# Order of the down product's chunks in an expert layer on one core

## The reference, cut to what matters

```
z = 2.0 * buf
z = z * jax.lax.rsqrt(jnp.mean(z * z, axis=-1, keepdims=True) + EPS) * norm_w[:, None, :]
g, u = jnp.split(jnp.einsum('ecd,ehd->ech', z, w13), 2, axis=-1)
y = buf + ALPHA * jnp.einsum('ech,edh->ecd', jax.nn.silu(g) * u, w2)
```

## Time and profile before

| what | value |
|---|---|
| median of 3 runs | 341.99 us (341.45 to 344.46) |
| the profiled execution, its own time | 343.51 us |
| its span, first to last instruction | 341.7 us |
| its mean granted TensorE clock | 0.925 of full speed |

### The profile page before, as it was taken

How to read it: one execution, slowest core, us unless ns; L and a number is a source line. 1 busy time by engine, 2 the same in 40 slices (tenths; PEclk the granted TensorE clock), 3 DMA queues, 4 the chain that set the end, 5 groups by cost and what they waited for, 6 DMA issues and landing times.

```text
span 341.7 us, 6143 instructions
## 1 busy us (share of the span) xinstructions
PE 285.1 (83%) x1893; PEld 226.0 (66%) x1893; DVE 203.8 (60%) x605; ACT 157.5 (46%) x442; POOL 141.6 (41%) x174
## 2 busy tenths in 40 slices
PE   8747889999979798988773939999999999999910
PEld 4624666776767575756562428989899898989910
DVE  2344787788798797978847223654737374564210
ACT  0013667777767575756633025353543535352210
POOL 9313233325545354544546700072433617153360
PEclk9975999999999999999955878999999999999985
DMA  7969700000000000050000181566585757661321
GB/s 246 272 153 304 278 3 0 2 1 12 27 4 25 11 18 18 18 119 24 21 18 28 54 227 26 125 130 175 91 213 105 177 127 141 155 115 11 32 26 17
DMA packets 24843, 30.32 MB, mean 89 GB/s; under 512 B 3346, under 2 KB 21560, under 8 KB 24692
## 3 DMA queue, kind: packets, MB, share of 16 engines
q1 hardware_dynamic: 18275, 21.45, 24.1%
q0 software_dynamic: 6288, 8.49, 12.0%
q10 hardware_dynamic: 256, 0.10, 0.1%
HBM read 19.61 MB, written 11.20 MB: 90 GB/s over the span
## 4 chain that ended last, share of the span: by engine, by line
PE 50%; ACT 13%; DMA 11%; DVE 10%; issue 8%; POOL 5%; ACTq 0%; POOLq 0%; DVEq 0%; SPq 0%
PE bank L541 12%; PE bank L436 6%; ACT kbd L625 6%; DMA zs<-slots 4%; PE bank L518 3%; PE bank L525 3%; PE bank L522 3%; PE bank L519 3%; PE bank L526 3%; DMA slots<-rows,slot 3%; PE bank L468 2%; DMA h_all<-ptok_sb 2%; ACT qT L627 2%; DVE mx L815 2%; PE bank L503 2%
## 5 line engine op out<-in xcount | busy, mean ns | idle before, releaser
L1042 POOL DMA_INDIRECT out_rows<-yw,tok x32 | 51.6, 1613 | 86.4 <-ACT yw L671 79.1
L541 PE MATMUL bank<-w_sb,hT 128*120 128x192 f32 x256 | 43.4, 328 | 1.1 <-DVE hT L928 0.7
L990 POOL TENSOR_TENSOR qk<-rc,rs 128x192 f32<-128x192 f32 x32 | 18.7, 602 | 60.6 <-DVE rs L831 60.6
L541 PEld LDWEIGHTS bank<-w_sb,hT 128*120 128x120 f32 x256 | 41.4, 183 | 2.5 <-issue 2.4
L928 DVE TENSOR_TENSOR hT<-sg,bank 128x480 f32<-128x480 f32 x32 | 20.8, 650 | 34.6 <-ACT sg L662 34.6
L1026 POOL DMA_INDIRECT slots<-rows,slot x32 | 32.3, 1010 | 9.9 <-issue 9.3
L662 ACT ACTIVATE sg<-bank 128x480 f32<-128x480 f32 x32 | 18.3, 571 | 32.7 <-PE bank L526 31.1
L671 ACT ACTIVATE yw<-yx,zs 120x192 f32<-120x192 f32 x32 | 12.8, 448 | 36.2 <-DVE yx L940 36.1
L625 ACT COPY kbd<-bank 32x288 f32<-32x288 f32 x64 | 24.8, 388 | 7.7 <-PE bank L476 6.5
L518 PE MATMUL bank<-z0h,wah 128*128 128x480 f32 x64 | 25.8, 403 | 0.0
L436 PE MATMUL bank<-kbd,qT 128*64 128x192 f32 x192 | 20.1, 347 | 6.4 <-ACT qT L627 6.0
(11 more groups left out here) (143 smaller groups left out, 658.7 us busy)
## 6 DMA issues: line engine op xcount, KB each, us to landing
rawa_sb<-in_w SPq DMA_DIRECT2D x8, 512.0 KB
rawb_sb<-in_w SPq DMA_DIRECT2D x16, 256.0 KB
w_sb<-in_w SPq DMA_DIRECT2D x8, 384.0 KB
slots<-zero_sb POOLq DMA_DIRECT2D x1, 3030.0 KB
zs<-slots SPq DMA_DIRECT2D x8, 378.8 KB
patch_sb<-in_patches SPq DMA_DIRECT2D x1, 1152.0 KB, 7.2
out_rows<-h_all SPq DMA_DIRECT2D x2, 432.0 KB, 5.6
h_all<-in_txt SPq DMA_DIRECT2D x2, 384.0 KB, 8.9
```

The lines of the kernel that those rows point to most:

```text
L541: mm = pe.matmul(bank[6 + c // 2][0:CR, (c % 2) * D:(c % 2 + 1) * D], hT[:, m, c * CR:(c + 1) * CR], w2_sb[:, par, m, :], start=(m == 0), ...
L1042: pool.indirect_dma_start(out=out, out_offset=bass.IndirectOffsetOnAxis(ap=tok[:, e, c:c + 1], axis=0), in_=yw[:, c, :], in_offset=None, b ...
```

## The change

The order in which the chunks of the down product are computed. Before: chunk 0 with m = 0 to 2, chunk 2 with m = 0 to 2, then m = 3 of chunk 0, m = 3 of chunk 2, then chunk 1 and chunk 3 whole. After: chunk 0 with m = 0 to 2, its m = 3, chunk 1, then chunk 2, then chunk 3. The waits are written by the part and the chunk: the wait for hT[3] stands ahead of chunk 0's m = 3 as before, the wait for the second bank to be free stands ahead of chunk 2's first matmul as before, and `s_down` is raised behind chunks 1 and 3 as before. Number, shape and operands of the matmuls are the same.

```diff
-                for c, parts in ((0, (0, 1, 2)), (2, (0, 1, 2)), (0, (3,)), (2, (3,)),
-                                 (1, (0, 1, 2, 3)), (3, (0, 1, 2, 3))):
+                for c, parts in ((0, (0, 1, 2)), (0, (3,)), (1, (0, 1, 2, 3)),
+                                 (2, (0, 1, 2, 3)), (3, (0, 1, 2, 3))):
                     if parts[0] == 0 and c == 0:
                         pe.wait_ge(s_hT, MH * e + 3)
                     if parts[0] == 3 and c == 0:
```

## The result

| | before | after |
|---|---|---|
| median | 342.19 us (4 runs) | 347.4 us (4 runs) |
| the profiled execution | 343.51 us, span 341.7 | 348.43 us, span 346.6 |
| ratio after to before | | 1.0219, interval 1.015 to 1.0288 |

The account below looks back on a forecast made before the run. TensorE was taken to set the pace in the expert stage. Stalls of 4.58 us less 0.61 us at the tail gave +3.97 us on the median of 341.99, so 346.0 us, 1.2% slower, range 342.9 to 348.4.

Parts of the forecast that it names:

- TensorE sets the pace, and the start of the product hangs on hT[2]: Expert stage: TensorE is busy almost throughout, 14.78 of 14.80 us in expert 1; the down product starts 0.13 us behind hT[2].
- The stall: Down product, seventh record: TensorE waits for hT[3], 0.72 to 0.76 us in experts 1 to 6, 0.19 in expert 0.
- passed on in full: Experts 0 to 6: each wait for hT[3] delays the next expert by its whole length, 4.58 us in sum.
- The tail: Expert 7: first bank announced 1.30 us earlier, less 0.69 us of waiting for hT[3], moves the end by -0.61 us.
- The load of the slots, "I take 0": Load of `zs` for experts 2 to 7: the earlier indirect DMAs were taken to change its length by 0.
- The bound of 0.35 us a load: Six `zs` loads: each at most 0.35 us shorter or longer, so -2.1 to +2.1 us in sum.
- Time of the wait that moved: Wait for the second bank, now mid-product: at most 3.2 us, at least nothing, expected nearer to nothing.
- the clock: TensorE's clock stays full; rival that it drops, one down product costing 5.4 us more, 351 us or above, chance 0.02.
- the first call's traffic may be through before `zs` begins: Argument for the rival with half given back: `zs` 0.35 us sooner in six loads, 343.9 us, chance 0.20.
- The rule of the Trainium skill: Shared DMA engines: the call moved in front of the `zs` load's end makes it later, sum nearer the upper end.
- worse: Rival: `zs` comes later by 0.35 us in its six loads, 348.1 us, chance 0.11.
- The rule on rotating banks: Down product: evacuating the first bank overlaps 8 matmuls, not 4, so the new order is better; counted alone, -1.30 us.

Follow-up runs that it names:

- With the stall gone: Kernel after, with VectorE making the low half of the second weight tile behind hT[3] and not ahead of it: ratio 1.0062 to the kernel before.
- -0.73 alone: Order of before in experts 0 to 6, new order in expert 7 only; six loads 30.26 us, ratio 0.9943 to the kernel before.
- the combination: Kernel before with hT[2] ahead of both low halves, late additions in experts 0 to 6, new order in expert 7 only: 342.59 against 346.63 us, ratio 0.989.

## Why the prediction was wrong

- *TensorE sets the pace, and the start of the product hangs on hT[2]*: right. Moving hT[2] forward gained 2.0 us in experts 1 to 6.
- *The stall*: forecast 0.72 to 0.76 us in experts 1 to 6, measured 0.65 to 0.71 (0.67 in the mean, 9.34 - 8.67), and 4.03 in place of 4.39 us in sum. The seventh record starts 0.06 us behind the end of hT[3] (231.54 + 0.65 = 232.19, and 232.25), not the 0.13 that the first record needs. In expert 0 +0.10 in place of 0.19.
- *It is passed on in full*: right. With the stall gone the rest was back at 8.67 us.
- *The tail*: forecast -0.61, measured -0.68, and -0.73 alone. The 0.07 is the same early start of the seventh record (326.96 + 0.65 = 327.61, and 327.67).
- *The load of the slots, "I take 0"*: this is the step that failed. It grew by 2.0, 2.8 and 2.1 us in the three profiles of after, against the mean of before. I had argued that the same number of calls falls into the load, give or take one, and gave that one no price. It is the effect, in each of six loads; the rows are below. Against the mean that takes in the 30.26 of the unchanged experts too (29.42) the growth is 1.9 us by the mean of after: the size is known to about half a microsecond, the sign is not in doubt.
- *The bound of 0.35 us a load*, from two rows, was too narrow: the second profile of after has 0.46 more a load than before's mean.
- *Time of the wait that moved, and the clock*: at 0 as taken; the 26 records behind the stall take 4.49 us in each expert, and the clock stayed full.

The busy time during the load of expert 5 (DMA share and GB/s last), in the kernel before:

```profile
283.37:287.99 4.62, 4.62 (x23) 4.00 (x22) 1.31 (x3) 3.02 (x4) 4.01 (x3) 1.00 0.93 191
```

and in the kernel after:

```profile
286.84:292.06 5.22, 5.22 (x26) 4.52 (x25) 1.31 (x2) 3.40 (x5) 4.61 (x3) 1.00 0.94 190
```

The rate is the same, and the engines are nearly full in both. 191 x 4.62 = 882 KB moved in the one and 190 x 5.22 = 992 KB in the other: 110 KB more, about one addition (120 rows of 768 bytes, 92 KB), in 0.6 us more. Which addition it is, GpSimd's calls of expert 5 show, in the kernel before:

```profile
282.65 1.58 POOL L1042 DMA_INDIRECT out_rows<-yw,tok  x1 [8.08 <-ACT yw L671]
284.53 1.59 POOL L1042 DMA_INDIRECT out_rows<-yw,tok  x1 [0.30 <-issue]
286.42 1.58 POOL L1042 DMA_INDIRECT out_rows<-yw,tok  x1 [0.30 <-issue]
```

and in the kernel after:

```profile
284.82 1.58 POOL L1042 DMA_INDIRECT out_rows<-yw,tok  x1 [9.19 <-ACT yw L671]
286.70 1.59 POOL L1042 DMA_INDIRECT out_rows<-yw,tok  x1 [0.30 <-ACT yw L671]
288.59 1.58 POOL L1042 DMA_INDIRECT out_rows<-yw,tok  x1 [0.30 <-issue]
```

In a quiet stretch the bulk of a call's traffic moves 2.3 to 3.3 us behind its start (last section). An estimate with this delay puts two calls into the load of before (285.0 to 286.0 and 286.8 to 287.8, the third from 288.7 behind its end at 287.99) and three into that of after (287.1 to 288.1, 289.0 to 290.0, 290.9 to 291.9, all ahead of its end at 292.06), the numbers that the bytes give. So "the first call's traffic may be through before `zs` begins", my argument for a shorter load, was wrong: it starts 1.6 us behind the issue of `zs` before the change, and 0.3 us behind it after the change.

I had a row that pointed there, a DMA share of 1.10, though for one microsecond only: over the whole of each load the share is 0.83 to 0.94 in the first profile of before, 0.91 to 0.99 in the first of after, and 0.57 to 0.65 with no additions. The rule of the Trainium skill ("DMA: Bandwidth & Descriptors", section "Issuing engines are not separate DMA queues") pointed the right way too: the trace agrees with it. I gave "worse" a chance of 0.11 where it should have been the forecast.

The sum with the measured terms: 4.03 + 0.10 - 0.68 + 2.3 (loads, mean of three profiles of after against two of before) = 5.8 us, 1.7% (5.3 us with the 1.9 of the wider mean). That lies within both intervals of the ratio and between the 5.2 and 6.2 us of the medians. What the ratios show over it (1.0207 and 1.0219) the runs don't settle.

The rule on rotating banks (the Trainium skill, "Perfetto Trace Analysis", section "Optimizing Tensor Performance"), as I read it in the prediction, would have had a gain here; the trace agrees in expert 7 alone, where the evacuation of the first bank is on the path. Both orders use two banks in turn, so the rule by itself doesn't choose between them.

## What to carry to other kernels

An order that looks odd may be there to cover a late operand: before making it tidy, list for each piece when its inputs are ready, and count how much work stands ahead of the last one. Where a change makes one engine finish early, follow what that starts: here it brought other traffic into a load that sat on the path, on DMA engines that were nearly full. The rate gives a rough price, 92 KB at 190 GB/s, 0.48 us an addition, a little over the 0.38 us measured; while the engines had room, one addition more cost nothing that showed. And an early finish pays only at the one place where someone waits for it; the combination takes it there alone.

## What the runs showed of the hardware

The traffic of an indirect DMA comes well after its instruction. In the quiet tail of the kernel before, GpSimd's first call of expert 7 starts at 326.67; the busy time in single microseconds (DMA share and GB/s last):

```profile
327.00:328.00 1.00, 0.00 (x0) 0.00 (x0) 0.00 (x0) 0.37 (x2) 1.00 (x1) 1.00 0.00 0
328.00:329.00 1.00, 0.00 (x0) 0.00 (x0) 0.00 (x0) 0.00 (x0) 0.69 (x2) 1.00 0.25 10
329.00:330.00 1.00, 0.00 (x0) 0.00 (x0) 0.00 (x0) 0.00 (x0) 1.00 (x1) 1.00 0.69 82
```

Nothing moves for 1.3 us at least, and most of it moves between 2.3 and 3.3 us behind the start of a call that the profile shows as 1.58 us long. So whether a call meets a load can't be read from where its bar stands; one has to add this delay.
